# First tokens of a LoRA-FFN kernel: three transfers instead of two, and the first weights split ahead of token half 1

## The reference

```python
xc  = einsum('bsi,boi->bso', x, L0_cond_weight[itok_B_3_7])      # x: (8, 256, 1024), weight: (8, 1024, 1024)
p   = softmax(xc @ W_router.T)                                   # 8 experts
top = the two largest p, divided by their sum; combine = 0 for the other experts
h   = einsum('nd,erd->ner', xc, A_stack) * combine[..., None]    # rank 16
out = x + xc @ W_base.T + b_base + 2.0 * einsum('ner,eor->no', h, B_stack)
```

## Time and profile before

| | us |
|---|---|
| median of 3 runs (397.47 to 397.65) | 397.62 |
| profiled execution | 397.48 |
| its span, first to last instruction | 395.7 |
| TensorE busy | 390.4 (99%) |
| VectorE busy | 301.7 (76%) |
| ScalarE busy | 184.0 (46%) |

### The profile page before, as it was taken

How to read it: one execution, slowest core, us unless ns; L and a number is a source line. 1 busy time by engine, 2 the same in 40 slices (tenths; PEclk the granted TensorE clock), 3 DMA queues, 4 the chain that set the end, 5 groups by cost and what they waited for, 6 DMA issues and landing times.

```text
span 395.7 us, 5686 instructions
## 1 busy us (share of the span) xinstructions
PE 390.4 (99%) x2186; PEld 332.5 (84%) x2186; DVE 301.7 (76%) x429; ACT 184.0 (46%) x281; POOL 39.9 (10%) x67
## 2 busy tenths in 40 slices
PE   7999999999999999999999999999999999999996
PEld 7888888888888888888888888888888888888885
DVE  4897966779699999974457786768868999998311
ACT  5877734748632444222146676256746224441000
POOL 0101100110000040021172000000000002201110
PEclk9999999999999999999999999999999999999999
DMA  7998872768430056485669877356083102642222
GB/s 260 397 352 287 309 279 84 262 214 297 157 106 0 28 181 181 169 282 197 217 215 368 339 244 241 108 174 234 17 274 113 40 0 83 189 156 81 80 80 80
DMA packets 21083, 72.96 MB, mean 184 GB/s; under 512 B 2816, under 2 KB 2832, under 8 KB 21056
## 3 DMA queue, kind: packets, MB, share of 16 engines
q1 hardware_dynamic: 15840, 55.58, 40.4%
q0 software_dynamic: 4928, 15.97, 11.4%
q10 hardware_dynamic: 288, 1.05, 0.7%
HBM read 64.20 MB, written 8.39 MB: 183 GB/s over the span
## 4 chain that ended last, share of the span: by engine, by line
PE 97%; DMA 1%; ACT 0%; DVE 0%; ACTq 0%; issue 0%
PE bank_x L783 30%; PE bank_x L787 15%; PE bank_y L768 9%; PE bank_y L770 9%; PE bank_y L769 9%; PE bank_x L770 8%; PE bank_x L769 8%; PE bank_x L768 8%; PE bank_y L827 2%; DMA raw<-x 1%; PE bank_y L847 0%; ACT x_hl L483 0%; DVE out_sb L577 0%; ACTq L340 0%; ACT wc_hl L483 0%
## 5 line engine op out<-in xcount | busy, mean ns | idle before, releaser
L783 PE MATMUL bank_x<-x_hl,wc_hl 128*128 128x512 f32 x512 | 128.9, 393 | 0.8 <-ACT wc_hl L483 0.8
L526 DVE TENSOR_TENSOR wc_hl<-raw,wc_hl 128x1024 fp32r<-128x1024 f32 x90 | 108.4, 1220 | 19.4 <-ACT wc_hl L465 19.4
L465 ACT CAST wc_hl<-raw 128x1024 fp32r<-128x1024 f32 x90 | 93.6, 1051 | 59.8 <-DVE raw L530 23.6
L783 PEld LDWEIGHTS bank_x<-x_hl,wc_hl 128*128 128x128 f32 x512 | 92.1, 189 | 18.0 <-ACT wc_hl L483 1.5
L787 PEld LDWEIGHTS bank_x<-x_hl,wc_hl 128*128 128x128 f32 x512 | 70.0, 190 | 5.1
L787 PE MATMUL bank_x<-x_hl,wc_hl 128*128 128x256 f32 x512 | 71.5, 282 | 0.0
L417 POOL DMA_DIRECT2D out<-out_sb x28 | 15.3, 545 | 250.5 <-DVE out_sb L577 229.2
L494 ACT COPY xc_low<-bank_x 128x256 f32<-128x256 f32 x64 | 23.6, 369 | 32.7 <-PE bank_x L787 32.7
L669 DVE TENSOR_TENSOR xp<-bank_x,xc_low 128x256 f32<-128x256 f32 x64 | 26.9, 420 | 15.5 <-ACT xc_low L494 14.7
L569 DVE SCALAR_TENSOR_TENSOR out_sb<-bank_x,bias_sb,out_sb 128x512 f32<-128x512 f32 x32 | 23.5, 746 | 18.1 <-PE bank_x L770 15.1
L770 PE MATMUL bank_x<-x_hl,wc_hl 128*128 128x512 f32 x96 | 37.4, 389 | 0.0
(11 more groups left out here) (86 smaller groups left out, 478.5 us busy)
## 6 DMA issues: line engine op xcount, KB each, us to landing
raw<-w_cond SPq DMA_DIRECT2D x62, 512.0 KB, 4.8
raw<-w_base SPq DMA_DIRECT2D x24, 512.0 KB, 5.7
out_sb<-x POOLq DMA_DIRECT2D x32, 256.0 KB, 5.5
raw<-x SPq DMA_DIRECT2D x14, 512.0 KB, 5.1
out<-out_sb POOLq DMA_DIRECT2D x28, 256.0 KB, 2.3
raw<-x ACTq DMA_DIRECT2D x2, 512.0 KB, 3.7
raw<-w_cond SPq DMA_DIRECT2D x4, 256.0 KB, 3.8
out<-out_sb SPq DMA_DIRECT2D x4, 256.0 KB, 2.0
```

What stands on the lines that cost most here:

```text
L465: nc.scalar.copy(split_dst(key, HI), split_src(key)).then_inc(hi_done, 1)
L526: nc.vector.tensor_tensor(split_dst(key, LO), split_src(key), split_dst(key, HI).bitcast(F32), ALU.subtract).then_inc(lo_done, 1)
L783: nc.tensor.matmul(ps[:], wc_hl[:, slot_of(s, t), HI, k], x_hl[:, s % 2, k].rearrange("p h n -> p (h n)"), start=(k == 0), stop=False)
```

## The change

X0 is now moved in two transfers of 256 KB with rows of 2 KB, and X1 (still one transfer of 512 KB with rows of 4 KB) is the third in ScalarE's queue. In `HI_PIECES` and `LO_PIECES` the first half of W0 (k = 0 to 3) goes ahead of the two pieces of X1. TensorE takes tile t = 0 in two steps of four k, each with its wide and then its narrow matmuls, where it had one step of eight.

```diff
-ACT_MOVES = [(X0, 0, 4), (X1, 0, 4)]
+ACT_MOVES = [(X0, 0, 2), (X0, 2, 4), (X1, 0, 4)]
 SP_MOVES = [(W0, 0, 4), (W0, 4, 8), (W1, 0, 4), (W1, 4, 8)]
-HI_PIECES = [(X0, 0, 2), (X0, 2, 4), (X1, 0, 2), (X1, 2, 4), (W0, 0, 2), (W0, 2, 4), (W0, 4, 8), (W1, 0, 4),
+HI_PIECES = [(X0, 0, 2), (X0, 2, 4), (W0, 0, 2), (W0, 2, 4), (X1, 0, 2), (X1, 2, 4), (W0, 4, 8), (W1, 0, 4),
              (W1, 4, 8)]
-LO_PIECES = [(X0, 0, 2), (X0, 2, 4), (X1, 0, 2), (X1, 2, 4), (W0, 0, 4), (W0, 4, 8), (W1, 0, 4), (W1, 4, 8)]
-
-START_STEPS = [(0, 0, 8), (1, 0, 4), (1, 4, 8)]
+LO_PIECES = [(X0, 0, 2), (X0, 2, 4), (W0, 0, 4), (X1, 0, 2), (X1, 2, 4), (W0, 4, 8), (W1, 0, 4), (W1, 4, 8)]
+
+START_STEPS = [(0, 0, 4), (0, 4, 8), (1, 0, 4), (1, 4, 8)]
```

## The result

| | before | changed |
|---|---|---|
| median, us (7 runs each) | 397.62 | 398.81 |
| profiled execution | 397.48 | 398.88 |
| its span | 395.7 | 397.1 |

The ratio is 1.0035, with a 95% interval of 1.0025 to 1.0045: slower by 1.2 to 1.4 us. The forecast of 397.7 was wrong, and so was its range up to 398.1.

What follows compares the result with a forecast made beforehand. TensorE's own work was taken to bound the kernel, its end moving with the early stretch. Order +0.03 and transfers +0.1 gave +0.13 on the median 397.62: 397.75, written as 397.7, range 397.3 to 398.1.

Steps and rivals of the forecast that it cites:

- What bounds the kernel: TensorE: waits of 1.2 and 0.8 us early, none after 6.83, so the end moves as tile 1's start moves.
- Parts 1 to 3: Start of ScalarE, VectorE, TensorE: new order of casts, lo pieces and matmuls starts tile 1 at 10.06, not 10.03: +0.03.
- Part 4: Token transfers at the start: X0 in 2 KB rows delays the tokens' stream and W0's first half by +0.1.
- the high end: Token transfers: 512 KB at 270 GB/s take 1.94, +0.63, time 398.3; as a rival, chance 0.05.
- W0's cover: ScalarE before the first matmul: 0.19 of W0's landing was hidden behind X1's casts; now a delay reaches TensorE.
- The fixed part paid anew: ScalarE's queue: each transfer pays 2.0 again, X1 lands at 7.3, k = 4 comes 0.5 later, 398.2; chance 0.01.
- Part 5: SyncE's weight reloads: w(0,5) issued at 8.9 instead of 7.4, early enough behind a late queue, cost zero.
- The clock: TensorE before its first real matmul: the pause drops its clock, costing 1.47, time 399.2; chance 0.03.

Runs made afterwards that it cites:

- order_only: The changed kernel with X0 and X1 put back to one transfer each, new order and TensorE steps kept: 397.83 us, ratio 1.0004.
- hold_sp: The changed kernel with SyncE, its index load included, held before its first transfer until X0's first transfer had landed: 400.36 us, ratio 1.0067.
- hold_late: The changed kernel with SyncE's first transfer held until X0's first transfer had landed, weight index loaded ahead of that wait: median 398.38 us, ratio 1.0015.
- moves_only: The kernel before with only X0 split into two transfers of 256 KB, X1 third, old order and TensorE steps: 398.94 us, ratio 1.0040.
- four_moves: The kernel before with X0 and X1 in two transfers of 256 KB each, 2 KB rows: median 398.83 us, ratio 1.0022.
- half_rows: The kernel before with X0 in two 256 KB transfers keeping 4 KB rows, partitions 0 to 63 then 64 to 127, X1 third: ratio 1.0074.
- odd_even: The kernel before with X0 in two 256 KB transfers keeping 4 KB rows, even partitions then odd ones, X1 third: ratio 1.0130.
- after_again: The changed kernel measured once more, with no further edit, against the kernel before: median 398.66 us, ratio 1.0028.
- before_again: The kernel before, unedited, profiled once more for the scatter of its landings: 397.41 us.

## Why the prediction was wrong, point by point

- **What bounds the kernel:** right. TensorE waits twice, and the span moved by what tile 1's start moved (1.4 and 1.42).
- **Parts 1 to 3, order on ScalarE, VectorE, TensorE:** right, in every link. From W0's landing to its first matmul 0.47 was forecast and 0.48 measured (7.54, 8.02); to k = 4, 2.35 and 2.35 (9.89); to tile 1, 3.88 and 3.91. The new order is worth nothing either way: +0.03 forecast, 1.0004 measured with order_only.
- **Part 4, the transfers: the step that failed.** +0.1 on W0's landing was taken, +0.63 was the high end, +1.36 was measured. Two faults. First, the term came from a cost per byte in full flow, as if a split changed nothing else. The split disturbed the flow itself: 234 GB/s, tokens 0.85 late with nothing beside them (hold_sp). The high end rested on a wrong reading too: 270 GB/s was not the worst stretch with 2 KB rows. From 6.0 to 7.0 the kernel before moved 203, and at that rate 512 KB take 2.58, which is +1.27 instead of +0.63. Second, "issued at 3.4" was kept as a constant. It was the end of an index load that ran beside the very transfers that were edited. It moved to 2.76, and earlier was worse (hold_late), by a mechanism that the runs don't show.
- That the order had taken away W0's cover (the 0.19 behind X1's casts) was seen, but it is not what decided: moves_only, with the old order, lost as much (1.0040). There TensorE waits for X1's landing at 7.06 and the casts behind it.
- **The fixed part paid anew:** its X1 landing, 7.3, is what was measured (7.33), its mechanism is not: X0's second transfer landed 1.0 after its first (3.41, 4.43), not 2.0. And it let W0 land at 6.18, and so priced itself at 0.5. The Trainium skill ("DMA: Bandwidth & Descriptors", section "Anatomy of one DMA — SWDGE (gpsimd) path"), cited for it in part 4, fits its 2.0 us to transfers that GpSimd issues. These are ScalarE's. The rival's own 2.0 is worked out from rows and stands without it.
- **Part 5, the reloads:** right. SyncE issued w(0,5) at 10.37 (8.9 forecast), 2.9 later than before, and it landed at 15.06 (15.02 before).
- **The clock:** right for the two profiles of the changed kernel (pauses of 0.91 and 1.93, no fall), though the pause was forecast at 0.66. It is only 0.91 in the first because the warm-up ended late there, at 7.12. The rival is real: it came in four_moves after a pause of 2.27, in half_rows after 2.80 and in odd_even after 3.72. One of the seven runs of the changed kernel took 400.1 and one of the ten of after_again 400.17, both at a mean clock of 0.995, where the others had 0.999 or 1.0; that these were such falls is likely, but they have no profile. The Trainium skill ("TensorE: Matmul & The Clock Gate", section "HAM oscillation — how this bites in real kernels") has long enough pauses re-throttle the array. The three falls agree with it; hold_sp, with 2.96 and no fall, shows that here the length alone did not decide.
- The range was too narrow because all its uncertainty hung on one number, the landing of the first weights, and that number's spread was taken from stretches that left out the dips of the kernel's own stream.

**Open:** why the engines fall to 192 to 282 GB/s from 3.25 to 4.50 in every run in which tokens move in transfers of 256 KB, against 406 to 416 where they move in two of 512 KB with 4 KB rows. The runs show that the split does it without weights beside it and that 2 KB rows aren't required and not harmless. In the changed kernel single packets stretch; in odd_even the share of the engines was only 0.71, so they also stood idle. What the packets or the engines wait for isn't shown, nor why an earlier issue of W0 makes the tokens later.

## What to carry to other kernels

When an edit touches the first transfers of a kernel, treat every landing behind them as unknown, not only the one that was split, and ask which engine's own small loads run beside them, since that sets when the next queue starts. Splitting an early transfer to have its first half sooner pays only if somebody waits for that half: here ScalarE had X0's first half cast 3.5 us before the weights it is multiplied with. A transfer issued earlier on a second queue is not one that lands earlier. And a high end for a transfer is read from the worst stretch that the trace has, all of it, not from a stretch chosen for another purpose.

## What the runs showed of the hardware that was not expected

- An index load of SyncE from HBM took 0.59 to 0.69 us in the six profiles in which it ran beside first transfers with 2 KB rows, and 1.32 to 1.73 in the five that begin with X0 in one transfer of 4 KB rows. The rows alone don't make it: with 4 KB rows in two transfers over 64 partitions each (half_rows, odd_even) it took 0.46.
- W0's first half landed 0.72 us sooner when issued 0.77 us later (hold_late). Its first packet started at 4.72, as in after_again (4.69), so 1.21 us after the issue and not 1.95.
- TensorE's 26 warm-up matmuls ended anywhere from 5.9 to 7.1 in the 14 profiles. It hangs on when their spacing falls from 0.21 to 0.12 us: at about 4.2 in hold_sp, not at all in before_again.
- ScalarE took 0.55 and 0.61 us to issue the two transfers over 64 partitions (half_rows, odd_even), and 0.37 to 0.49 for those over 128 in the other runs. The third transfer behind the two of 64, over 128 partitions, took 0.60 as well, so the number of its own partitions is not what sets it.
